# Second attention of a fused two-layer block: q and k stacked twice over the partitions, scores as 64-row pairs

## The reference, cut to what matters

```python
# second attention: 32 query heads, 8 key/value heads, head size 16
q = (query @ Wq).reshape(b, sq, 32, 16).transpose(0, 2, 1, 3)   # sq = 256
k = (key @ Wk).reshape(b, sk, 8, 16).transpose(0, 2, 1, 3)      # sk = 512
v = (value @ Wv).reshape(b, sk, 8, 16).transpose(0, 2, 1, 3)
scores = einsum('bhqd,bhkd->bhqk', q, repeat(k, 4)) * 128 ** -0.5
out = einsum('bhqk,bhkd->bhqd', softmax(scores), repeat(v, 4)) @ Wo
```

## Time and profile before

| what | value |
|---|---|
| median of 3 runs | 1134.33 us (1128.93 to 1134.96) |
| the profiled execution's own time | 1125.34 us |
| its span in the trace | 1123.5 us |
| mean granted TensorE clock | 0.967 of full speed |
| PE busy | 1012.8 us, 90% |
| weight loads busy | 877.3 us, 78% |
| VectorE busy | 665.8 us, 59% |
| ScalarE busy | 482.3 us, 43% |
| GpSimd busy | 376.5 us, 34% |
| score loop of the second attention | 913.9 to 1055.9 us |

### The profile page before, as it was taken

The page is one execution under the profiler, slowest core; times in us unless marked ns, Lnnn a source line. Parts: engine busy times, 40 slices in busy tenths (PEclk is TensorE's granted clock), DMA queues, the critical chain, the costliest instruction groups (busy, mean ns, idle before and its releaser), DMA issues. The chain is left out here.

```text
span 1123.5 us, 18617 instructions
## 1 busy us (share of the span) xinstructions
PE 1012.8 (90%) x6780; PEld 877.3 (78%) x6780; DVE 665.8 (59%) x1128; ACT 482.3 (43%) x938; POOL 376.5 (34%) x251
## 2 busy tenths in 40 slices
PE   2989999999999999999999999998898579999964
PEld 1979889898898898989889898897776357777543
DVE  5467467457556646745745674673486546667396
ACT  2356336436535634643643563372131125555311
POOL 4306503711730640361173065032892300000054
PEclk9989999999999999999999999999998689999986
DMA  5001100100200110110020011000531173121000
GB/s 172 35 1 57 39 1 27 67 0 0 93 0 0 56 37 0 47 46 0 0 93 0 0 56 56 0 1 1 171 102 38 38 205 63 29 56 29 1 1 37
DMA packets 29617, 46.49 MB, mean 41 GB/s; under 512 B 3216, under 2 KB 12048, under 8 KB 29584
## 3 DMA queue, kind: packets, MB, share of 16 engines
q1 hardware_dynamic: 29008, 46.03, 13.5%
q10 hardware_dynamic: 576, 0.00, 0.0%
HBM read 41.83 MB, written 4.19 MB: 41 GB/s over the span
## 5 line engine op out<-in xcount | busy, mean ns | idle before, releaser
L446 DVE TENSOR_TENSOR ptL<-tbank,ptH 128x512 fp32r<-128x512 f32 x192 | 132.3, 689 | 84.5 <-ACT ptH L330 84.5
L330 ACT ACTIVATE ptH<-tbank 128x512 fp32r<-128x512 f32 x192 | 115.9, 604 | 109.2 <-PE tbank L554 108.9
L281 POOL TENSOR_TENSOR oTL<-o_norm,oTH 128x512 fp32r<-128x512 f32 x32 | 41.3, 1291 | 347.1 <-ACT oTH L350 347.1
L554 PE MATMUL tbank<-ident,probs 128*128 128x128 f32 x864 | 132.2, 276 | 16.6 <-DVE ptL L446 12.3
L459 DVE TENSOR_REDUCE negmax<-score 128x1 f32<-128x768 f32 x128 | 119.5, 949 | 19.5 <-PE score L74 19.5
L417 DVE TENSOR_REDUCE sumsq<-probs 128x2 f32<-128x256 f32 (+1 forms) x80 | 42.1, 526 | 142.3 <-ACT probs L325 71.8
L356 ACT ACTIVATE probs<-score,negmax 128x768 f32<-128x768 f32 x128 | 115.7, 904 | 15.4 <-DVE negmax L459 15.4
L72 PE MATMUL obank<-ptH,vH 128*128 128x256 f32 x384 | 121.8, 317 | 0.0
L554 PEld LDWEIGHTS tbank<-ident,probs 128*128 128x128 f32 x864 | 97.9, 140 | 26.9 <-DVE ptL L446 15.1
L276 POOL TENSOR_TENSOR rnorm<-sumsq,neg_half 128x2 f32<-128x2 f32 (+1 forms) x80 | 71.9, 901 | 111.3 <-DVE sumsq L419 111.3
L73 PE MATMUL score<-wkvL,kvT_hi 128*128 128x256 f32 x384 | 108.7, 283 | 0.0
(11 more groups left out here) (250 smaller groups left out, 2467.9 us busy)
## 6 DMA issues: line engine op xcount, KB each, us to landing
wqo_stage<-in_wq SPq DMA_DIRECT2D x9, 1024.0 KB, 5.7
wqo_stage<-in_wo SPq DMA_DIRECT2D x8, 1024.0 KB, 5.3
wkv_stage<-in_wkv SPq DMA_DIRECT2D x9, 512.0 KB, 6.5
a_qS<-q_scratch SPq DMA_DIRECT2D x32, 128.0 KB, 3.8
ctx_stage<-in_ctxT SPq DMA_DIRECT2D x2, 1024.0 KB, 14.0
kS<-k_scratch SPq DMA_DIRECT2D x32, 64.0 KB, 2.1
q_scratch<-part SPq DMA_DIRECT2D x8, 256.0 KB, 4.0
wqo_stage<-in_down_w SPq DMA_DIRECT2D x3, 512.0 KB, 4.8
```

The source lines that it names most:

```text
L330: act.activation(out, tbank[c % 2][:], ACT.Copy, scale=scale).then_inc(t_hi, 1)
L446: i = dve.tensor_tensor(out, tbank[c % 2][:], f32(hi), ALU.subtract)
L554: i = pe.transpose(tbank[c % 2][:, n * P:(n + 1) * P], block_in, S.ident[:])
```

## The change

q and k are loaded twice, into partitions 0 to 63 and 64 to 127, with twice as many DMAs; the two memsets of the zero halves and the waits for them go. The two matmuls of `scores` take the lower 64 partitions for the first 128 query rows and the upper 64 for the second. The four transposed-score matmuls of a unit go first, bank 0 in the lower and bank 1 in the upper 64 partitions, in alternation; the four matmuls that add the negative maxima, unchanged in shape, come behind them in a function of their own, `add_maxima`, with the wait for the reductions. `negmax` has room for 4 units. `times_v`, `transpose_o` and `finish_quad` move one unit later within the quad.

```diff
@@ ffn0
-            sp.wait_ge(k_zeroed, 1)
             for s in range(2):
                 S.load_k(sp, s, s)
...
-            pool.memset(f32(S.kS[64:P, :, :]), 0.0).then_inc(k_zeroed, 1)
-            pool.wait_ge(k_zeroed, 1)
@@ attn1
-    negmax = sb("a_negmax", [P, 4], f32r)
+    MB = 4
+    negmax = sb("a_negmax", [P, 2 * MB], f32r)
-    STACK = 8 * 16
+    STACK = 16 * 16
+    H = P // 2
+    low, high = slice(0, H), slice(H, P)
@@ attn1, sync
-            sp.wait_ge(zeroed, 2)
             def load_q(g, s):
-                for n in range(4):
-                    heads = q_dram[n // 2].rearrange("(h d) n -> d h n", d=D1)
+                for n in range(8):
+                    heads = q_dram[n // 2 % 2].rearrange("(h d) n -> d h n", d=D1)
@@ attn1, gpsimd
-            pool.memset(f32(qS[64:P, :, :, :]), 0.0).then_inc(zeroed, 1)
-            pool.wait_ge(zeroed, 2)
@@ attn1, vector
-                    if v % GRP == 3 and (not first or v >= GRP):
-                        finish_quad(i, r - 1, v // GRP - 1)
+                    if v % GRP == 0 and (not first or v >= 2 * GRP):
+                        finish_quad(i, r - 2, v // GRP - 2)
...
-            finish_quad(TURNS - 1, QUADS * TURNS - 1, QUADS - 1)
+            for w in (QUADS - 2, QUADS - 1):
+                finish_quad(TURNS - 1, QUADS * (TURNS - 1) + w, w)
@@ attn1, tensor
-                    q = b * SQ + t * P
-                    pe.matmul(score[t][:], qS[:, s, j, q:q + P], kS[:, s, b * SC:(b + 1) * SC],
+                    q, rows = b * SQ + t * P, (low, high)[t]
+                    pe.matmul(score[t][:], qS[rows, s, j, q:q + P], kS[rows, s, b * SC:(b + 1) * SC],
                               start=True, stop=True).then_inc(pe_s, 1)
+
+            def add_maxima(n, v):
+                pe.wait_ge(s_max, 2 * n + 2)
+                for half in range(2):
+                    bank = scoreT[v % 2][:, 512 * half:512 * (half + 1)].rearrange("p (k q) -> p k q", k=2)
+                    for t in range(2):
+                        m = negmax[:, 2 * (v % MB) + t:2 * (v % MB) + t + 1]
+                        x = pe.matmul(bank[:, :, t * P:(t + 1) * P], m.to_broadcast([P, P]),
+                                      ident_r[:].unsqueeze(1).to_broadcast([P, 2, P]), start=False, stop=t == 1)
+                x.then_inc(pe_sT, 1)
 
             def scores_T(n, v, first):
...
-                pe.wait_ge(s_max, 2 * n + 2)
-                for kt in range(0, SCT, 2):
...
+                for k in range(2):
+                    for half, rows in enumerate((low, high)):
+                        key = b * SC + (2 * half + k) * P
+                        pe.matmul(scoreT[v % 2][:, 512 * half + k * SQ:512 * half + (k + 1) * SQ], kS[rows, s, key:key + P],
+                                  qS[rows, s, j, b * SQ:(b + 1) * SQ], start=k == 0, stop=False)
...
                     scores_T(n, v, first)
+                    add_maxima(n, v)
                     if not first or v >= GRP:
-                        if v % GRP == 1:
+                        if v % GRP == 2:
                             times_v(r - 1, (v // GRP - 1) % QUADS, i if v >= GRP else i - 1, first)
-                        if v % GRP == 2:
+                        if v % GRP == 3:
                             transpose_o(r - 1, (v // GRP - 1) % 2)
```

More of the change, by code:

```diff
@@ L696, in ffn0 @@
     pe_v, v_done = sem("pe_v"), sem("v_rows_done")
-    k_zeroed, stats3_done = sem("k_zeroed"), sem("stats3_done")
+    stats3_done = sem("stats3_done")
     w_in = {n: sem(f"{n}_in") for n in ("gate", "affine")}
@@ L1375, in maxima @@
                     dve.wait_ge(pe_s, 2 * n + t + 1)
-                    dve.tensor_reduce(negmax[:, 2 * (v % 2) + t:2 * (v % 2) + t + 1], score[t][:], AX.X, ALU.max,
+                    dve.tensor_reduce(negmax[:, 2 * (v % MB) + t:2 * (v % MB) + t + 1], score[t][:], AX.X, ALU.max,
                                       negate=True).then_inc(s_max, 1)
@@ L1450, in scores_T @@
                     pe.wait_ge(s_exp, n - 1)
-                pe.wait_ge(s_max, 2 * n + 2)
-                for kt in range(0, SCT, 2):
[L1453 to L1458, removed]
-                        key = b * SC + (kt + k) * P
-                        x = pe.matmul(bank[:, k * SQ:(k + 1) * SQ], kS[:, s, key:key + P],
-                                      qS[:, s, j, b * SQ:(b + 1) * SQ], start=False, stop=k == 1)
-                x.then_inc(pe_sT, 1)
+                for k in range(2):
[3 more added lines that the diff above has]
+                                  qS[rows, s, j, b * SQ:(b + 1) * SQ], start=k == 0, stop=False)
             def times_v(r, w, i, first):
```

## The result

The kernel after takes **1143.74 us** (median of 4 runs, 1143.23 to 1150.79), the kernel before beside it on the same chip 1131.63 us: ratio 1.0126, interval [1.0082, 1.0169]. I had forecast 1137.6 us and no clear change; it is slower by 12 us (medians) to 14 us (ratio). The 1143.7 us still lies at the end of my range of 1127 to 1144 us, but that range started from 1134.3 us for the kernel before. Counted from the kernel before it, the slowdown is above the range's upper end of +10.

A forecast was written before the change was run, and what follows sets the result against it. The loop was taken as bound by TensorE and VectorE in alternation. 0.8 - 3.0 + 7.5 - 2.0, with refills 0, gave +3.3 us: 1137.6 us against 1134.3, range 1127 to 1144.

The forecast's parts named there:

- Part 1: `ffn0`: twice the k loads delay GpSimd's chunk 5 by 3.6 us and TensorE's start by 0.8 us: +0.8 us.
- part 2: Normalisation ahead of q's matmuls: without the memset of `qS`, VectorE's second tile is no longer slowed: -3.0 us.
- Part 3: Before the first score: twice the q loads, ahead of the stores that ScalarE's last evacuation waits for: +7.5 us.
- rival B: q loads before the first score are bound by the issue, not the DMA rate: sum -4.2, 1130.1 us; chance 0.12.
- Part 4: Score loop: pairs run side by side but changes of shape cost time; -2 us in all.
- the walk: Step-by-step timing of TensorE and VectorE over one quad of the loop: 8.44 us after the change, 8.54 before.
- The change of shape: TensorE switching between 64- and 128-row matmuls, twice a unit: 0.19 us each, from drain and open weight load; bounds 0 to 0.22.
- Rival C: Loop: the weight loads of a pair come one after the other; loop +1.5 us, sum +6.8, 1141.1 us; chance 0.18.
- Rival A: Loop: changes of shape cost nothing, VectorE bounds, 7.93 us a quad; sum -5.7, 1128.6 us; chance 0.2.
- Rival D: Refills in the loop come late if 1.5 MB take over 15.5 us; at 18 us sum +18, 1152 us; chance 0.07.
- -0.1 us for 15 quads: Loop: each quad falls from 8.54 to 8.44 us, won in the unit with `times_v`; applied to 15 quads.
- for the first units, which run at half clock as before: Loop's first units: half clock lasts as before, and the change gains 0.5 us there.

The follow-up runs named there:

- e1: The kernel after with ScalarE's `copy_o` one unit later; ratio 1.0124 to the kernel before.
- e3: The kernel after with `times_v`, `transpose_o` and `finish_quad` back in their units of before; ratio 1.0065 to the kernel before.
- e4: The kernel before with q and k loaded twice and no two memsets, scores still over 128 rows, so counted twice; ratio 1.0052 to the kernel before.
- e7: e3's kernel with the maxima added over 64 rows, which leaves out half of them; ratio 0.9926 to the kernel before.
- e8: e3's kernel with the q loads of the lower and upper partitions in turn; ratio 1.0081 to the kernel before.
- e11: e3's kernel, unchanged, profiled once more; one run, 1134.84 us.
- e12: The kernel after with the transposed scores of the first 6 units made twice; ratio 1.0102 to the kernel before.
- e5: e3's kernel with q tile 1's stores ahead of group 0's loads and group 1's loads behind all stores; ratio 0.9983 to the kernel before.
- e2: The kernel before with only `times_v`, `transpose_o` and `finish_quad` moved one unit later; ratio 1.0044 to the kernel before.

## Why the prediction was wrong

**Part 1 (+0.8) and part 2 (-3.0).** Part 2 held: -2.9 us by the instructions that it named, and 5.2 to 5.5 us in place of 8.34 in all 11 profiles with the memset late or gone. Part 1 gave +1.0 us, and GpSimd's chunk came 3.6 us later as forecast, but its 1.0 us isn't clear of the spread: `ffn0` took 95.9 to 97.6 us in the five profiles with single k loads and 95.5 to 100.0 in the nine with doubled ones, 0.7 us more in the mean.

**Part 3 (+7.5), the mechanism right, the size only roughly.** The stores stand behind 16 loads in place of 8. ScalarE's wait grew by 5.7 us in the profile of the kernel after, and by 7.9 to 9.1 in seven other kernels with the doubled loads in the old order (e1, e3, e4, e7, e8, e11, e12). I had sized it by one rate, 155 GB/s, and that rate isn't fixed: with a share at or above 1 the DMA engines moved 128 and 182 GB/s in two successive stretches of 7.5 us in e4, 174 and 220 in the kernel after. So the sign that I gave for rival B, a rate above 155, did come and says nothing. Rival B is refuted by what it forecast, no delay at all: the 16 loads were issued in 7.6 us, and the store came 5.7 to 9.1 us late. For all three parts together e4 gives +5.9 us [+4.0, +7.8]; I had 5.3.

**Part 4, the middle of the loop, held.** A quad takes 8.4 us, as the walk had it, -0.9 us over units 8 to 48 (-1.0 was forecast). The change of shape costs what was read off: from the last 64-row matmul's start to the first 128-row one it is 0.20 us where two of 128 rows are 0.117 apart, and that one's record is 0.38 in place of 0.28 us for its weights in the open, 0.19 us together. The rule on draining of the Trainium skill, TensorEngine Tiling (Array Packing), section Key Properties, agrees with the 0.09 us of it. Rival C is refuted: the two matmuls of a pair start 3 ns apart and the pairs 0.114 us, so their weight loads run side by side. Rival A's condition is refuted by the same 0.19 us; its price of 7.93 us a quad was never measured alone (e7's 7.7 us has the paired maxima in it). Rival D didn't come: no refill was late, that is, no score inside the loop waited for DMA in any of these kernels; only the first score of e5 did.

**The step that failed** is part 4's "-0.1 us for 15 quads". It is a walk over a quad in the middle, where VectorE has the maxima and `finish_quad` to do, and I took it for the quads of the last turn as well. The move of `times_v` cost nothing in that walk, and I closed it with "`copy_o` and the exponentials come later by one `times_v`, inside ScalarE's idle half", read off the loop's mean. The move of the products cost 5.0 us in the kernel before (e2) and about 7 in the kernel after, and the last turn grew by 8.0 us where -0.4 was forecast. ScalarE's idle half does cover the later copy for three turns. In the fourth VectorE makes six weight splits between the maxima of the first units; `times_v` had given TensorE work during one of these, and one unit later it no longer does, so three pauses of TensorE stand where there was one. In the kernel after, half clock made them dearer. The sentence on `copy_o` is wrong for this turn too, since VectorE waited 6.1 us behind the copy, but e1 shows that it is not where most of the time went. This step is 7 of the 9 to 11 us that the forecast of +3.3 lacks (+12.1 by the medians, +14 by the ratio).

**The second miss** is "for the first units, which run at half clock as before". They ran so for 18.6 us and not 6.3, +3.9 us over units 0 to 8 where -0.6 was forecast. 64-row pairs with 128-row maxima lasted long in five of six profiles. e4, which pauses before the first score as long and has 128-row scores, was back in 7.4 us, and e5, which pauses for 5.2 us only, in 17.7; so it isn't the pause. The pairs as such cost +1.5 us [-1.2, +4.1] by e3 over e4 where I had -2. That the shapes are the reason is a pattern over 14 profiles; why e3 once took 9.0 us, and whether more work or another mix brings the clock back, stays open. The Trainium skill, TensorE: Matmul & The Clock Gate, Part 1, says that activity releases the throttle and that the number of slow matmuls varies from run to run of one kernel; the 9.0 and 19.1 us of e3 and e11 agree with the second. In e11 TensorE had no pause from 919.91 to 934.31 us and the clock stayed at half all the while; the first statement alone doesn't account for that.

## What to carry to other kernels

A stage that looks uniform in its mean may carry extra work in one turn: for an edit in a loop, walk the turn with the most work in it. Ask there what the moved work had covered on the other engines, and not only who now waits for it. Time won on one engine by packing is worth little while another takes turns with it (0.1 us a quad here), and the transfers that the packing needs are paid at once (5.9 us, the saved memset already taken off). Look for gains first at where a queue's order lets one transfer wait for another, and at what slows the way to the loop: two edits there (the order of the loads, a later memset), with no change to the loop, were timed at -11 us.

## What the runs showed of the hardware that I had not expected

- With 64-row pairs the granted clock (1.2 in place of 2.4 GHz) lapsed 1 or 2 times more in the loop in all eight such profiles, after pauses of TensorE of 1.4 and 1.5 us in the kernel after and of 1.1 us in e3. With 128-row scores it never did in six profiles, e2 among them, where TensorE pauses 1.31 and 1.45 us in the last turn as well.
- When the clock comes back is not fixed by the kernel: 9.0 and 19.1 us after the first score in two executions of e3's kernel; and between q's first matmul and the first store, 5.1 or 6.7 to 6.8 us in 11 profiles with the same q matmuls and no early memset.
- A DMA share at or above 1 doesn't tell the rate: it was 128 to 220 GB/s in stretches of 7.5 us of q loads. The order in which the loads of 128 KB fill the two halves of the partitions made no difference (e8, 21.7 us against 20.9 to 22.1 in the like kernels, 18.7 in the kernel after).
